# GNN layer with GAT on one Trainium2 core: node tiles and items found inside the edge stage, and h1 turned one bank earlier

## The reference

```python
h = jnp.maximum(_layernorm(x, axis=-1), 0.0)
# L0: aggregate edges at their destination, then an MLP
out1 = segment_sum(edge_attr, col); cnt = segment_sum(ones, col)
out2 = where(cnt > 0, segment_max(edge_attr, col), 0); out3 = out1 / maximum(cnt, 1)
f = concatenate([h, out1, out2, out3, u[batch]], axis=1)
x = x + relu(f @ W1 + b1) @ W2 + b2 + h
# L1: two graph attention layers on relu(layernorm(x)), 4 heads and 1 head, with self loops
h = maximum(_layernorm(x), 0.0)
x = x + gat(elu(gat(h)))
```

## Time and profile before

| | us |
|---|---|
| runs of the kernel before (three) | 6609.26, 6611.48, 6618.94; median 6611.48 |
| the profiled execution, own time | 6614.09 |
| its span in the profile | 6612.3 |
| busy: PE, PEld | 4628.9 (70%), 3413.7 (52%) |
| busy: DVE, ACT, POOL | 4352.8 (66%), 2950.7 (45%), 3469.3 (52%) |

### The profile page before, as it was taken

The page is one execution under the profiler, slowest core; times in us unless marked ns, Lnnn a source line. Parts: engine busy times, 40 slices in busy tenths (PEclk is TensorE's granted clock), DMA queues, the critical chain, the costliest instruction groups (busy, mean ns, idle before and its releaser), DMA issues. The chain is left out here.

```text
span 6612.3 us, 102298 instructions
## 1 busy us (share of the span) xinstructions
PE 4628.9 (70%) x22725; PEld 3413.7 (52%) x22853; DVE 4352.8 (66%) x12524; ACT 2950.7 (45%) x7934; POOL 3469.3 (52%) x3679
## 2 busy tenths in 40 slices
PE   0056655999996777777777777767777777777772
PEld 0044444888884555555555555445555555555551
DVE  7489997666665666666666666775555555555557
ACT  5044443222222666666666666544344334344440
POOL 6200000111113777777777777357777777777770
PEclk9878887999997888888888888878888878888885
DMA  1299998333333444444444444444444444444447
GB/s 39 73 353 399 398 402 310 108 109 108 106 111 88 120 121 120 121 120 120 120 120 120 120 120 120 105 125 110 110 110 110 110 110 110 110 110 110 110 110 244
DMA packets 366549, 965.22 MB, mean 146 GB/s; under 512 B 102255, under 2 KB 194134, under 8 KB 341351
## 3 DMA queue, kind: packets, MB, share of 16 engines
q0 software_dynamic: 168928, 459.50, 26.2%
q1 hardware_dynamic: 190456, 453.15, 19.1%
q10 hardware_dynamic: 7056, 51.38, 2.0%
HBM read 696.71 MB, written 267.03 MB: 146 GB/s over the span
## 5 line engine op out<-in xcount | busy, mean ns | idle before, releaser
L579 POOL DMA_INDIRECT rows<-table_d,idx x3328 | 3150.8, 947 | 1113.3 <-issue 903.6
L640 PE MATMUL pG<-rows,onehot 128*128 128x264 f32 (+1 forms) x6656 | 2154.6, 470 | 599.6 <-issue 341.3
L868 DVE TENSOR_TENSOR acc<-acc,pG 128x264 f32 (+1 forms) x3328 | 1417.7, 426 | 966.1 <-PE pG L640 588.0
L640 PEld LDWEIGHTS pG<-rows,onehot 128*128 128x128 f32 x6656 | 1471.2, 233 | 1127.0 <-issue 455.1
L732 ACT ACTIVATE rows<-rows 128x64 f32<-128x64 f32 (+1 forms) x4480 | 1249.9, 368 | 0.0
L725 ACT ACTIVATE onehotT<-pQ 128x1024 bf16<-128x1024 f32 (+1 forms) x512 | 442.4, 864 | 1290.6 <-PE pQ L612 1290.6
L714 ACT ACTIVATE onehot<-pQ 128x1024 f32<-128x1024 f32 (+1 forms) x512 | 441.0, 861 | 527.1 <-PE pQ L597 523.9
L1163 PE MATMUL pH<-hT_pre,w1h 128*128 128x256 f32 x1568 | 434.4, 433 | 219.8 <-ACT pre L1101 211.3
L1221 DVE SCALAR_TENSOR_TENSOR run<-run,same_e,ea 128x96 f32<-128x96 f32 x1567 | 491.6, 314 | 3.6 <-DMA ea<-in_ea 2.9
L1221 DVE SCALAR_TENSOR_TENSOR run<-run,cut_e,ea 128x96 f32<-128x96 f32 x1567 | 491.5, 314 | 0.1
L1163 PEld LDWEIGHTS pH<-hT_pre,w1h 128*128 128x128 f32 x1568 | 329.9, 218 | 304.2 <-ACT pre L1101 229.6
(11 more groups left out here) (299 smaller groups left out, 4822.0 us busy)
## 6 DMA issues: line engine op xcount, KB each, us to landing
rows_d<-run SPq DMA_DIRECT2D x98, 1536.0 KB, 11.2
ea<-in_ea SPq DMA_DIRECT2D x98, 768.0 KB, 13.6
rows<-table_d,idx POOLq DMA_INDIRECT x3328
pre_d<-pre ACTq DMA_DIRECT2D x49, 1024.0 KB
pre_in<-pre_d SPq DMA_DIRECT2D x49, 1024.0 KB, 5.2
tab<-tab_d SPq DMA_DIRECT2D x64, 392.0 KB
hrow_c<-table_d SPq DMA_DIRECT2D x98, 256.0 KB, 3.3
table_d<-g_rows SPq DMA_DIRECT2D x49, 260.0 KB
```

What stands on the lines that cost most here:

```text
L579: g.indirect_dma_start(out=rows[:, at.par, k, 0:XF + H], out_offset=None, in_=table, in_offset=bass.IndirectOffsetOnAxis(ap=idx[:, at.par, ...
L640: mm = pe.matmul(pG[(k + 2 * at.par) % 4][:, 0:W], onehot[:, k, :], rows[:, at.par, k, :], start=True, stop=True)
L868: v.tensor_tensor(to, to, pG[(k + 2 * at.par) % 4][:, 0:W], ALU.add).then_inc(added, 1)
```

## The change

The stage `structure` is gone, and the order is now `setup`, `edge_chains`, `masks`, `node_mlp`. What structure did is woven into `edge_chains`, at fixed groups g of DVE's walk and fixed steps n of ACT and PE:

- `last_i` is loaded by ACT's queue; POOL converts it; PE spreads it after the bias product; ACT copies the four pieces.
- All 98 counts are ACT's, COUNTS = 3 in each of steps 0 to 32, between its evictions. DVE's 49 counts are gone.
- DVE converts the counts of batch b (`whole_tiles`) before groups 13, 23, 31, 41, 51, 59, 69, and compares (`edges_of_tile`) five groups later, before 18, 28, 36, 46, 56, 64, 74. `le` is BF16 now. The small instructions stand before groups 74, 78, 81, 84 and 87, PE's part of them before steps 37, 39, 41 and 42.
- POOL issues the 98 and the 39 gathers during the walk. The rows of destinations lie in the space in which the item lists come later (`keep["lists"]`).
- The node tile of each item comes from one transpose of `jcol` in place of four products with a row of 1664, and `jrow` is stored as 13 rows of 128.
- `pE`, `pC`, `pB` and the spread share three PSUM banks `pU`; `place` lies in `last_all`.

In `node_mlp` PE's products for the last bank (kk = 3) come after the turn of h1, DVE adds that bank after its copy of h1T, and ACT makes h1 before `hidden(at, 1)`.

```diff
@@ edge_chains, ACT
+            for i, (c0, w) in enumerate(SPREADS):
+                a.wait_ge(spread, i + 1)
+                a.activation(last_all[:, c0:c0 + w], pU[i % 2][:, 0:w], ACT.Copy).then_inc(spread_copied, 1)
             normal(0)
...
-                evict(n, range(2, HC - 1))
+                evict(n, range(2, 4))
+                count_tiles(n)
+                evict(n, range(4, HC - 1))
...
+            def count_tiles(n):
+                for j in range(COUNTS * n, min(COUNTS * n + COUNTS, NT)):
+                    if j:
+                        a.wait_ge(counted_act, j)
+                    a.activation(junk_act[:, :], last_all[:, :], ACT.Sign, bias=node_above[:, j:j + 1], scale=-1.0,
+                                 accum_out=signs[:, j:j + 1]).then_inc(counted_act, 1)
@@ edge_chains, POOL
+            for b in range(NBL):
+                g.wait_ge(full_ready, b + 1)
+                if b >= 2:
+                    g.wait_ge(rows_used, b - 1)
+                for q in range(JB):
+                    g.indirect_dma_start(
+                        out=rows[:, b % 2, q, :], out_offset=None, in_=tiles_of("dst"),
+                        in_offset=bass.IndirectOffsetOnAxis(ap=full_i[:, b * JB + q:b * JB + q + 1], axis=0),
+                    ).then_inc(rows_in[b % 2], 16)
+            g.wait_ge(rows_used, NBL)
+            g.wait_ge(icol_ready, 1)
+            for name, of in (("D", "dst"), ("Nx", "dst_next"), ("S", "src")):
+                for k in range(KT):
+                    g.indirect_dma_start(
+                        out=item_lists(s, keep)[name][:, k, :], out_offset=None, in_=tiles_of(of),
+                        in_offset=bass.IndirectOffsetOnAxis(ap=icol_i[:, k:k + 1], axis=0),
+                    ).then_inc(keep["items_in"], 16)
+            g.wait_ge(keep["items_in"], 16 * 3 * KT)
             g.wait_ge(heads, 1)
@@ edge_chains, DVE
+            def whole_tiles(b):
+                js = slice(b * JB, (b + 1) * JB)
+                v.wait_ge(counted_act, JB * (b + 1))
+                v.tensor_scalar(full_i[:, js], signs[:, js], 0.5, ET / 2, ALU.mult, ALU.add).then_inc(full_ready, 1)
+
+            def edges_of_tile(b):
+                js = slice(b * JB, (b + 1) * JB)
+                v.wait_ge(rows_in[b % 2], 16 * JB * (b // 2 + 1))
+                v.tensor_tensor(le[:, :, :], rows[:, b % 2, :, :], node[:, js].unsqueeze(2).to_broadcast([P, JB, P]),
+                                ALU.is_le).then_inc(rows_used, 1)
+                v.wait_ge(rows_used, b + 1)
+                v.tensor_reduce(part[:, js], le[:, :, :], AX.X, ALU.add).then_inc(parts, 1)
+                v.wait_ge(parts, b + 1)
...
             for e in range(EW):
                 g, k = e // G, e % G
+                if k == 0:
+                    between(g)
@@ masks, SP
-            sp.dma_start(dr["jrow"], keep["jrow"][:, :]).then_inc(stored, 16)
+            sp.dma_start(dr["jrow"].rearrange("o (k p) -> (o k) p", p=P), keep["jT"][:, :]).then_inc(stored, 16)
@@ node_mlp, PE
-                    for kk in range(KK):
-                        for h in range(2):
-                            cols = slice((2 * kk + h) * P, (2 * kk + h + 1) * P)
-                            for i in range(2):
-                                mm = pe.matmul(pM1[kk][:, h * N2:(h + 1) * N2], w1e[:, i, cols], fT[:, at.par, i, :],
-                                               start=False, stop=(i == 1), skip_group_check=True)
-                        mm.then_inc(m1_ready, 1)
+                    for kk in range(KK - 1):
+                        products(at, kk)
                 if n is None or n >= 1:
                     pe.wait_ge(h1_ready, prev.n * 2 + 2)
...
+                if mlp:
+                    products(at, KK - 1)
@@ node_mlp, ACT
-                if mlp:
-                    hidden(at, 1)
                 if n is None or n >= 1:
                     normal(prev, 1, x1[:, prev.par, :, :], h1[:, :, :], h1_ready)
                 if mlp:
+                    hidden(at, 1)
                     hidden(at, 2)
@@ node_mlp, DVE
                     add_first(at, 2)
-                    add_first(at, 3)
                 if back:
                     v.wait_ge(gt_ready, prev.n + 1)
                     v.tensor_copy(h1T[:, :, :].rearrange("p i n -> p (i n)"), pG[:, :]).then_inc(gt_copied, 1)
+                if mlp:
+                    add_first(at, 3)
```

More of the change, by code:

```diff
@@ L340, in _ @@
                 v.wait_ge(tr, n + 1)
-                out = (keep["last"], keep["src"])[q]
+                out = (keep["last"], src)[q]
                 v.tensor_copy(out[:, k0 * P:(k0 + w) * P],
@@ L987, in edge_chains @@
         fix = sb("fix_e", [P, 2, EF])
[L988 to L989 removed]
+        pU = [c.enter_context(nc.psum_tensor(f"pU{i}", [P, 512], F32)) for i in range(3)]
+        pE = pU[0][0:EF, :].rearrange("p (m e) -> p m e", m=4)
+        pC = pU[1][:, 0:2 * EF].rearrange("p (m f) -> p m f", m=2)
+        pB = pU[2][:, 0:HC]
+        last_i = sb("last_i", [1, ET], I32)
+        last_f = sb("last_f", [1, ET])
+        ones = sb("ones_row", [1, P])
+        junk_act = sb("junk_act", [P, ET], BF16)
+        node = sb("node", [P, NT])
+        node_i = sb("node_i", [P, NT], I32)
+        node_above = sb("node_above", [P, NT])
+        signs = sb("signs", [P, NT])
+        full_i = sb("full_i", [P, NT], I32)
+        le = sb("le", [P, JB, P], BF16)
+        part = sb("part", [P, NT])
+        end = sb("end", [P, NT])
+        nodesT = sb("nodesT", [NT, P])
+        prevT = sb("prevT", [NT, P])
+        cntT = sb("cntT", [NT, P])
+        endm = sb("endm", [P, NT])
+        shift = sb("shift", [P, P])
+        shift_i = sb("shift_i", [P, P], I32)
+        bi = sb("bi", [NT, 1], I32)
+        lo = sb("lo", [NT, 1], I32)
+        lof = sb("lof", [NT, 1])
+        pidx_i = sb("pidx_i", [P, 1], I32)
+        tj = sb("tj", [NT, 1])
+        titem = sb("titem", [NT, NI], I32)
+        begun = sb("begun", [NT, NI], BF16)
+        ones_b = sb("ones_b", [P, 1], BF16)
+        jcol = sb("jcol", [P, KT])
+        tcol = sb("tcol", [P, KT], I32)
+        icol = sb("icol", [P, KT])
+        icol_i = sb("icol_i", [P, KT], I32)
+        rows = keep["lists"][:, 0:2 * JB * P].rearrange("p (b q e) -> p b q e", b=2, q=JB)
         w1h = sb("w1h", [P, 2, HID])
@@ new lines, in tile_row, with between @@
+            def tile_row():
+                v.wait_ge(jcol_turned, 1)
+                done(v.tensor_copy(keep["jT"][:, :], pU[1][0:KT, 0:P]))
+            def between(g):
+                if g in FULL_AT:
+                    whole_tiles(FULL_AT[g])
+                if g in EDGES_AT:
+                    edges_of_tile(EDGES_AT[g])
+                if g == END_AT:
+                    ends()
+                if g == NODES_AT:
+                    ends_of_nodes()
+                if g == BEGUN_AT:
+                    begun_tiles()
+                if g == ITEMS_AT:
+                    items()
+                if g == ROW_AT:
+                    tile_row()
```

315 lines of the change are left out of this document (117 added, 198 removed).

## The result

| | us |
|---|---|
| changed kernel, four runs | median 6416.15 (6413.18 to 6426.62) |
| kernel before, four runs | median 6611.26 (6609.26 to 6618.94) |
| ratio | 0.9708, 95% interval 0.9696 to 0.9719 |
| forecast | 6418, range 6394 to 6475 |
| profiled span | 6411.4, before 6612.3 |

A forecast was written before the change was run, and what follows sets the result against it. DVE's chain was taken to bound the edge stage, with transfers right behind. Structure's -232.5 and the added costs summed to -193.3 us, own time 6614.1 to 6420.8, as a median 6418; range 6394 to 6475.

The forecast's parts named there:

- Chain of DVE: Edge stage: work moved into DVE's chain is all on the path, +35.5, lost overlap +1.7, gathers hindering DVE +3.
- Gathers: POOL in the edge stage: 14 take 17.4 us, land some 2 later, DVE asks after 37.6; cost 0.
- a gather grows by that at most: POOL beside DVE's chain: a two-input chain instruction delays a gather by at most its own 0.31 us.
- rival 4: POOL's gathers starve beside DVE's unpausing chain, one gather a group of 7.52 us: 7094 us; chance 0.05.
- Does a gather hold DVE up?: Edge stage: gathers cost DVE's chain +3 us, between 0 and 7, at most 0.05 each.
- Rival 2: Edge stage: each gather holds DVE off for its whole 0.94 us, 129 in all: 6544 us; chance 0.03.
- Rival 3: Edge stage: the counts don't fit on ACT, 33 steps each lack 2.2 us, +73: 6491 us; chance 0.05.
- Transfers: Edge stage: the gathers' transfers against rest from comparisons, 0 net, between -2.9 and +29 us.
- Rival 1: Edge stage: transfers become the bound, +29 at full price: 6447 us; chance 0.10.
- Start: Start of the edge stage: last_i's load competes with the first loads, +1 us, between 0 and 8.
- Node MLP: MLP step: wait of 0.75 goes, waits of 0.3 and 0.35 come; -2 us, bounds -19 to +14.
- Rival 5: Node MLP: the turn does nothing, step stays 18.69 us, time 6420; inside the forecast, which with it has chance 0.77.

The follow-up runs named there:

- e4: Changed kernel with one tiny 128x1 copy in DVE's chain after 4, 8 and 12 edges of groups 13 to 86: 6458.14 us, ratio 0.9765.
- e5: Changed kernel with comparisons three groups behind the gathers' start in place of five: 7803.81 us on the second chip, ratio 0.9871.
- e8: Changed kernel with three x loads issued right behind the first edge load and the bias added before group 2: 7713.44 us on the second chip, ratio 0.9764.
- e7: Changed kernel with ACT issuing the load of last_i only after its wait for the masks: 7722.19 us on the second chip, ratio 0.9771.
- e11: Changed kernel with x loaded first and the first six comparisons seven groups behind the gathers' start in place of five: 6403.29 us, ratio 0.9692.
- e6: Changed kernel with four counts a step on ACT in place of three, for 25 steps in place of 33: 6422.90 us, ratio 0.9720.
- e9: Changed kernel with DVE's comparisons and reductions replaced by one ACT instruction per node tile: 7712.55 us on the second chip, ratio 0.9750.
- e10: Changed kernel with x loaded first and six of seven comparisons on ACT, the last on DVE: 6401.07 us, ratio 0.9684.
- e1: Kernel before with the node MLP's change alone: 6595.46 us against 6612.30, ratio 0.9975.
- e2: Changed kernel with the node MLP of before: 6431.77 us, ratio 0.9732.
- e3: Changed kernel with ACT making the second bank's hidden rows ahead of the rows h1, as before: 6480.06 us, ratio 0.9803.

## Why the forecast was right, and where it was wrong

*Chain of DVE, forecast +40.2, measured +40.5.* The bound was read rightly: the chain bounds the stage, and what is put into it lies on the path. Comparison and reduction took 2.02 each, as in structure, with bf16 output and input:

```profile
L1159 DVE TENSOR_TENSOR le<-k_lists,node 128x1792 bf16<-128x1792 int32 x7 | 14.1, 2021 | 3.6 <-DMA k_lists<-in_dst,full_i 3.6
L1162 DVE TENSOR_REDUCE part<-le 128x14 f32<-128x1792 bf16 x7 | 14.1, 2020 | 0.2
```

*Gathers, forecast no wait for their rows, measured 3.6.* Here a step failed: "a gather grows by that at most", 0.31. It grew by 0.99 in the mean and by 7 at worst. The rows of structure had a gather blocked by one long instruction that ended; a chain of short ones without a break blocks it until the chain's next break, for the longest the end of a group (e4, e5). This is rival 4's mechanism, and in its place too. It costs little because two gathers in a batch are caught, not all fourteen as the rival had it: from gather to gather it is 1.93 + 0.30 = 2.23 in the mean, not 4.1. The landing was too small as well: some 2 behind the last gather, as structure had shown with its queues nearly idle (1.5 to 1.9), and 5.8 to 7.3 in the four batches for which DVE waited here. A batch of 30.4 to 31.8 and such a landing fill the lead of 37.6 us, with nothing left over. The zero in the sum was luck: one more group end in a batch costs 7 us, and that came two and three times in e8 and e7. e11 shows what makes it safe.

*Does a gather hold DVE up?* The seven comparisons of the changed kernel say nothing on this, as no gather runs beside them: each comes 5.8 us or more after its batch. The links of the chain do. Those that begin while a gather is under way, short or long, follow each other at 0.229 us like those without one, and the 3134 links take 0.310 in the mean, before 0.314. Rival 2 falls. The rule of the Trainium skill (SBUF — State Buffer, Who interferes with whom) that the exclusion holds both ways agrees here for the gather alone, as in the rows of before.

*ACT, forecast 0, measured 0.* The wait for x was free to use (55.2 left), and e6 shows room for more. Rival 3 falls.

*Transfers, 0 net, measured +2.5.* They were nearer than the sum used: e9 and e10 took DVE work out, and 13 to 20 us came back as waits for ea. That fits the forecast's reasoning that the comparisons gave the queues their rest. Rival 1 did not come about in this kernel, but it stands close behind.

*Start, forecast +1, measured +7.2, inside the bound of 8.* The step failed in looking at last_i as the one that waits. It was last_i that made others wait: u's issue, and x behind it on SP (e7, e8).

*The next stage, forecast 0, measured +3.2.* The mask stage's first DVE instruction follows POOL's last gather by 6.9 us before and 7.2 now, the MLP's first load only by 3.0. The 232.5 that I took off ran up to that first instruction, and so held an entry into the mask stage of 6.9 that stays; what went was the entry into the MLP of 3.0. The end of the edge stage itself became 1.0 shorter.

*Node MLP, forecast -2, measured -14.7.* The mechanism was right (no wait for h1T, 0.45 for h1, 0.31 for the last hidden rows), the size was not: "8.78" for the end of the last bank's loads was 8.55, and the second product began at 10.39 and not 10.54 (10.58 before). That is 0.19 of the 0.30 a step; the other 0.11 are the first sixteen loads of the second product, 3.32 for 3.43. In these rows the loads behind an idle time are 0.11 to 0.15 shorter, so a wait costs less than its idle time; why they are shorter was not tried. 0.30 x 47 = 14, inside the bound of -19. Rival 5 falls by e1 and e2.

So +10 in the edge and mask stages and -13 in the MLP met in the sum, and 5 of scatter went the same way as the MLP. The range held each of them. That the total lies only 2 us off (7.5 profile against profile) is luck; that it lies in the range is not. Two of the forecast's own signs of being wrong came true: DVE waited for gathered rows, and the MLP step is under 18.4.

## What to carry to other kernels

A stage that leaves engines idle can dissolve into one that a single chain bounds, and then only what goes into that chain counts; read first how far the next bound is, since the transfers took back half of what e9 removed. A POOL gather beside an unbroken chain of two-input DVE instructions has no fixed duration: give its result a lead for the worst batch, here 39.0 us for 14 gathers and 7 for the landing (e7), or 3.3 us a gather, or put the chain's breaks where the gathers are. In front of a queue of large loads, put the small loads of single numbers last, and when an order is turned on one engine, price the engine that feeds it (e3: 55 us).

## What was not expected of the hardware

- A gather of 0.94 us takes up to 8.04 (e5) beside the chain of 0.31 us instructions that start every 0.23, and ends 0.9 us after the chain's next break. Six links are 1.37, and a gather of 1.07 with its gap 1.37: the two run in step, which may be why so few gathers are caught. One copy of 128x1 every 1.9 us brings the mean from 1.93 to 1.06.
- One load of 1568 single numbers on ACT's queue made an issue on SP's queue 12.93 us long in place of 7.31.
- The rows of a batch of gathers landed 1.5 to 1.9 us behind the last gather at a DMA share of 0.16, and 5.8 to 7.3 behind it at 0.98.
- A second chip ran the MLP alike and the attention 1290 us slower, gathers of L386 at 0.948 us each against 0.947, with a granted clock of 0.77 in place of 0.84. What holds it there was not tried.
